# Values cut in two and set among the turns, keys before queries, the low-rank product before the last values

## Chip, cores and metric

One core of a Trainium2 chip runs the whole program. The metric is device time in microseconds (us) of that core, the median of several runs. Engines: TensorE (PE; its weight loads are listed as PEld), VectorE (DVE), ScalarE (ACT), GpSimd (POOL), and SyncE (SP), which issues the DMA transfers here.

## The reference

The input x is (2, 1024, 512), float32: 2048 tokens. What is computed:

```
xn = layernorm(x)
q  = xn @ Wq                      # 32 heads of 16
k,v = xn @ Wkv                    # 8 groups of 16 each, k and v interleaved
s  = softmax(causal(q k^T) / 4) v, @ Wo + bo
gate, up = xn @ gate_w + low rank (16), xn @ up_w + low rank (16)
g  = silu((silu(gate) * up) @ down_w + low rank (16))
out = x + s * g
```

## The kernel before

**Chunks.** The 2048 tokens are four chunks of 512 (c = 0 to 3); chunks 0 and 1 are batch 0, chunks 2 and 3 batch 1. For each chunk TensorE turns the normalised x (`turn_x`, four "turns" of four transposes each, line 1026). ScalarE rounds each turned block out of PSUM (`round_x`, line 1311) and copies it whole (`copy_x`, line 1318); for chunks 2 and 3 GpSimd forms the rest, x minus its rounding (`low_x`, line 631). Projections (`project`, lines 306 to 308) multiply in three products, high by high, high by low, low by high, and so need that rest of all four blocks of the chunk. Values (`value`, line 1062) and the product of x with the low-rank factors (`low`, line 1077) are plain float32 products of the whole copy. A key projection is block KEYS_BLOCK (4) of a chunk, a query projection one of blocks 0 to 3.

**Steps and slots.** Two streams are woven on every engine by `interleave`: attention, in slots, and background, in steps. A turn is one step, a projection, a low-rank product and the values of a chunk are four each. The 24 steps up to `("proj", 1, 0)` come ahead; the next 46 are spread over the 40 slots before the first attention round; then it is one step a slot. In this text steps are counted behind those 24: low(0) is steps 1 to 4 in both kernels. From slot 10 on each second slot or so holds a pair of score products (`score_pair`, line 1241) of query and key tiles, whose row maxima VectorE takes (`maximum`, lines 1809 and 1812) out of three PSUM banks; TensorE waits there for a bank to be read. After the last pair of a half VectorE splits the maxima (`split_max`, lines 1819 to 1825), and they are turned by TensorE (line 1248), copied by ScalarE (line 1553) and put into q by DMA (line 968).

**Banks.** Background results go to two PSUM banks in turn. `take_bank` makes TensorE wait until the result that lay in the bank before has been read: a turn by ScalarE's two copies, a value by its one copy (line 1343), a projection or low-rank product by ScalarE's rounding (line 1335 or 1354) and then VectorE's subtraction (line 1631 or 1636).

**Round trip by DRAM.** Projections, values and the low-rank product are stored to DRAM (lines 749, 754, 760) and read back in another layout. All issues stand in one order on the SP queue, and an SP wait holds what is behind it. `load_x_a` (line 768) waits for both stored low-rank products and issues six reads; the FFN's hidden stage needs them. The reads of k and q for attention group 1 (lines 949 and 952) wait for every projection up to the newest that they need, among them the keys of chunk 3; TensorE's score pairs of group 1 wait for those reads. They stand at slot 41 of the SP stream.

**Order around the change,** from step 1 (before): low(0) 1-4; value(0) 5-8; value(1) 9-12; turns of chunk 2, 13-16; queries (0,1) 17-20; keys of chunk 2, 21-24; value(2) 25-28; turns of chunk 3, 29-32; low(1) 33-36; queries (1,1) 37-40; keys of chunk 3, 41-44; value(3) 45-48; queries (0,2) 49-52; then the hidden stage (line 1099). SP's `background` stores each result behind its steps; `load_x_a` comes ahead of the store of the keys of chunk 3. In the GpSimd stream `low_query_weights(2)` and `low_of_low` (line 640, two operations) follow the four `low_x` of chunk 2.

Of the kernel before, what the change touches and what calls it, by code (L numbers as in the profile page):

```python
# [19 lines left out]
H, G = 32, 8  # L20
# [83 lines left out]
LEADING = [(c, blk) for c in range(2) for blk in (KEYS_BLOCK, 0)]  # L104
BESIDE = {2: (0, 1), 3: (1, 1)}
AFTER = [(0, 2), (1, 2), (0, 3), (1, 3)] + [(c, blk) for blk in range(NBLK - 1) for c in (2, 3)]
PROJECTED = LEADING + [p for c in BESIDE for p in (BESIDE[c], (c, KEYS_BLOCK))] + AFTER
BESIDE_HIDDEN = AFTER[1:]
QUERY_TILES = [[[0], [1], [2], [3]]] * 2

# [8 lines left out]
REST = 2  # L119


STEPS = dict(turn=1, proj=KT, value=TT, low=KT, hidden=2 * KT, down_fold=2, rest=REST, down=NH + 1, out=KT)

# [39 lines left out]
    return out_behind(t)  # L163


def bank_order():

    for c in range(2):
        for k in range(KT):
            yield "turn", c, k  # L170
    for c, blk in LEADING:
        yield "proj", c, blk
    yield "low", 0, 0
    for c in range(2):
        yield "value", c, 0
    for c in BESIDE:
        for k in range(KT):
            yield "turn", c, k
        if c == 3:
            yield "low", 1, 0  # L180
        yield ("proj", *BESIDE[c])
        yield "proj", c, KEYS_BLOCK
        yield "value", c, 0
    for c, blk in AFTER[:SOON]:
        yield "proj", c, blk
    for h in range(NH):
        for c in range(NCH):
            yield "hidden", h, c
            if c == 1:
                yield "proj", *AFTER[SOON + h]  # L190
    for h in range(NH):
        yield "down_fold", h, 0
    yield "rest", 0, 0
    for t in range(NT):
        yield "down", t, 0
        if out_behind(t) is not None:
            yield "out", out_behind(t), 0
    for t in range(NT - TT, NT):
        yield "out", t, 0
# [111 lines left out]
def layer(nc, x, Wq, Wkv, Wo, bo, gate_w, up_w, down_w, low_a, low_b, low_a_down, low_b_down, out):  # L311
# [5 lines left out]
    with ExitStack() as ctx:  # L317
# [203 lines left out]
        def wait_filled(engine, key):  # L521
            engine.wait_ge(filled, NUMBER[key] + 1)

        def projection(c, blk):
            return PROJECTED.index((c, blk))

        def read_out(kind, a, b):


            if kind == "down" and a < SPLIT_DOWN:  # L530
                return (y_left, a + 1), (y_right, a + 1)
            if kind == "out" and a < SPLIT_OUT:
# [5 lines left out]
            return dict(turn=(xT_copied if a else xT_lo, KT * a + b + 1), proj=(p_lo, (kind == "proj" and projection(a, b)) + 1), value=(v_copied, a + 1),  # L538
                        low=(x_a_lo, a + 1), down_fold=(d_lo, a + 1), down=(y_done, a + 1),
                        out=(r1_done, a + 1))[kind],  # L540

# [37 lines left out]
        def _(pool):  # L579
# [74 lines left out]
            def background():  # L654
# [15 lines left out]
                yield NUMBER_STEPS["value", NCH - 1, 0] - done  # L670
                done = NUMBER_STEPS["value", NCH - 1, 0]
                for i in range(2):
                    low_weight(0, i)
                for h in range(NH):
# [43 lines left out]
        def _(sp):  # L718
# [31 lines left out]

            def store_value(c):
                b, t0 = divmod(c * C, T)
                sp.wait_ge(v_copied, c + 1)
# [87 lines left out]
            def background():  # L841
# [7 lines left out]
                        load_first()  # L849
                yield STEPS["low"]  # L850
                store_x_a(0)
                for c in range(2):
                    yield STEPS["value"]
                    store_value(c)
                for c in BESIDE:
                    yield KT * STEPS["turn"]
                    for n in range(4 * (c - 2), 4 * (c - 2) + 4):
                        load_raw(n)
                    if c == 3:
                        yield STEPS["low"]  # L860
                        store_x_a(1)
                    yield STEPS["proj"]
                    store_projection(*BESIDE[c])
                    if c == 3:
                        load_x_a()
                    yield STEPS["proj"]
                    store_projection(c, KEYS_BLOCK)
                    yield STEPS["value"]
                    store_value(c)
                for c, blk in AFTER[:SOON]:  # L870
                    yield STEPS["proj"]
                    store_projection(c, blk)
# [142 lines left out]
        def _(pe):  # L1015
# [38 lines left out]
                        mm.then_inc(filled, 1)  # L1054
                    yield 1

            def value(c):
                pe.wait_ge(xT_copied, KT * (c + 1))
                out_ = take_bank(("value", c, 0))
                for t in range(TT):  # L1060
# [3 lines left out]
                    if t == TT - 1:  # L1064
                        mm.then_inc(filled, 1)
                    yield 1

# [117 lines left out]
            def background():  # L1185
# [4 lines left out]
                for c, blk in LEADING:  # L1190
                    yield from project(c, blk)
                yield from low(0)
                for c in range(2):
                    yield from value(c)
                for c in BESIDE:
                    for kt in range(KT):
                        yield from turn_x(c, kt)
                    if c == 3:
                        yield from low(1)
                    yield from project(*BESIDE[c])  # L1200
                    yield from project(c, KEYS_BLOCK)
                    yield from value(c)
                for c, blk in AFTER[:SOON]:
                    yield from project(c, blk)
                for h in range(NH):
# [97 lines left out]
        def _(act):  # L1303
# [8 lines left out]

            def copy_x(c, kt):
                if c >= 2:
                    wait_filled(act, ("value", c - 2, 0))
                elif c:
                    act.wait_ge(xT_lo, KT * c + kt + 1)
                nc.scalar.activation(xT[:, c % 2, kt], bank_of(("turn", c, kt))[:, :], ACT.Copy).then_inc(xT_copied, 1)
# [19 lines left out]
            def copy_value(c):  # L1338
                key = ("value", c, 0)
# [22 lines left out]
            def round_weight(h, i):  # L1362
                n, hp = 2 * h + i, rows[h]
                if n == 0:
                    wait_filled(act, ("value", NCH - 1, 0))
# [55 lines left out]
            def background():  # L1421
# [24 lines left out]
                    round_query_weights(blk)  # L1446
                yield STEPS["low"]
                round_x_a(0)
                for c in range(2):
                    yield STEPS["value"]  # L1450
                    if c:
                        root(3)
                    copy_value(c)
                for c in BESIDE:
                    for kt in range(KT):
                        yield STEPS["turn"]
                        round_x(c, kt)
                        copy_x(c, kt)
                    if c == 3:
                        yield STEPS["low"]  # L1460
                        round_x_a(1)
                    yield STEPS["proj"]
                    split_projection(*BESIDE[c])
                    yield STEPS["proj"]
                    split_projection(c, KEYS_BLOCK)
                    yield STEPS["value"]
                    copy_value(c)
# [112 lines left out]
        def _(dve):  # L1580
# [130 lines left out]
            def background():  # L1711
# [16 lines left out]
                normalise_x(3)  # L1728
                yield 2 * STEPS["value"]
                for c in BESIDE:  # L1730
                    for kt in range(KT):
                        yield STEPS["turn"]
                    if c == 3:
                        yield STEPS["low"]
                        low_of_x_a(1)
                    yield STEPS["proj"]
                    low_projection(*BESIDE[c])
                    yield STEPS["proj"]
                    low_projection(c, KEYS_BLOCK)
                    yield STEPS["value"]  # L1740
# [149 lines left out]
```

## Time and profile before

| | us |
|---|---|
| median of 3 runs | 932.41 (930.68 to 933.27) |
| the profiled execution, its own time | 935.35 |
| its span, first to last instruction | 933.6 |
| PE busy | 885.7 (95%) |
| DVE busy | 576.6 (62%) |
| ACT busy | 488.9 (52%) |
| POOL busy | 345.4 (37%) |

"Busy" is time in which an engine ran an instruction; waits are listed with what ended them. The granted clock of TensorE is 1.00 at full speed (2.4 GHz) and 0.50 at the lower level (1.2 GHz); its mean over the span is 0.984. Over the span the 16 DMA engines moved 137 GB/s.

### The profile page before, as it was taken

The page shows a single profiled execution, that of the slowest core. Times are in us where ns is not written, and L with a number is a line of the kernel's source. Part 1 is how long each engine was busy: PE and PEld are TensorE (multiplying, and loading weights), DVE is VectorE, ACT ScalarE, POOL GpSimd, SP SyncE. Part 2 cuts the span into 40 slices and gives each one's busy share as a digit, 9 for nine tenths or more (in the row PEclk, how much of TensorE's full clock was granted, in tenths as well). Part 3 has the DMA queues.
Part 4 walks back from the last instruction along what each step waited for, and adds up shares of the span by engine and source line. Part 5 has one row for each costly group of instructions (what it writes and reads, how often), then busy time and mean ns, then how long its engine had stood idle before and what let it go on. Part 6 is the DMA issues. An engine that isn't in the chain of part 4 may idle for free.

```text
span 933.6 us, 21793 instructions
## 1 busy us (share of the span) xinstructions
PE 885.7 (95%) x8415; PEld 641.2 (69%) x8415; DVE 576.6 (62%) x1674; ACT 488.9 (52%) x1002; POOL 345.4 (37%) x340
## 2 busy tenths in 40 slices
PE   3989799999999999999999999999999999999997
PEld 3754467676767676767677776665677777777885
DVE  7666466657566666666757566677766666661136
ACT  3441365656565656565656565656555454545211
POOL 4170236363636363635353545432021313130133
PEclk9998899999999999999999999997999999999999
DMA  8466525253525343434343434347465546434663
GB/s 278 158 190 170 150 71 154 61 148 84 144 72 149 81 143 85 135 87 130 94 130 91 132 97 133 97 136 222 128 224 158 160 138 186 160 98 136 211 207 134
DMA packets 143094, 129.80 MB, mean 139 GB/s; under 512 B 37360, under 2 KB 115920, under 8 KB 140816
## 3 DMA queue, kind: packets, MB, share of 16 engines
q1 hardware_dynamic: 142992, 128.41, 47.4%
q8 instruction: 68, 1.11, 0.5%
q14 instruction: 34, 0.28, 0.1%
HBM read 74.09 MB, written 53.74 MB: 137 GB/s over the span
## 4 chain that ended last, share of the span: by engine, by line
PE 86%; DVE 4%; DMA 3%; SPq 2%; ACT 2%; issue 2%; DVEq 0%; ACTq 0%
PE bank L1099 28%; PE bank L1142 15%; PE o L1277 14%; PE s L1241 9%; PE st L1260 8%; PE bank L306 3%; PE bank L307 2%; PE bank L308 2%; DMA sums<-scratch_o 1%; PE bank L1108 1%; PE bank L1077 1%; PE bank L1062 1%; SPq L968 1%; DMA scratch_k<-proj_hi 1%; PE bank L1122 1%
## 5 line engine op out<-in xcount | busy, mean ns | idle before, releaser
L1543 ACT ACTIVATE prob<-st 128x512 f32<-128x512 f32 (+1 forms) x640 | 323.3, 554 | 265.3 <-PE st L1260 263.7
L1809 DVE CUSTOM_DVE_ANT_0 junk<-s,mask 128x128 bf16<-128x128 f32 (+3 forms) x512 | 229.2, 487 | 81.4 <-PE s L1241 81.0
L1812 DVE TENSOR_REDUCE part_max<-s 128x1 f32<-128x512 f32 x256 | 164.1, 682 | 127.7 <-PE s L1241 127.2
L1241 PE MATMUL s<-k,q 64*128 64x512 f32 (+3 forms) x768 | 157.6, 376 | 15.4 <-DMA q<-scratch_q 6.6
L1099 PE MATMUL bank<-x_hi,w_hi 64*128 64x512 f32 (+1 forms) x704 | 151.0, 414 | 3.9 <-DVE proj_lo L1629 2.3
L604 POOL TENSOR_SCALAR_AFFINE_SELECT prob<-prob 128x512 f32<-128x512 f32 x128 | 81.1, 646 | 182.6 <-ACT prob L1543 182.5
L1277 PE MATMUL o<-prob,v 128*32 128x512 f32 (+3 forms) x1536 | 145.9, 498 | 0.0
L1099 PE MATMUL bank<-x_lo,w_hi 64*128 64x512 f32 (+1 forms) x704 | 143.6, 392 | 0.0
L1099 PE MATMUL bank<-x_hi,w_lo 64*128 64x512 f32 (+1 forms) x704 | 142.8, 390 | 0.0
L1260 PE MATMUL st<-q,k 64*128 64x512 f32 (+3 forms) x768 | 141.7, 347 | 1.0 <-ACT prob L1543 0.5
L1241 PEld LDWEIGHTS s<-k,q 64*128 64x128 f32 x768 | 80.9, 187 | 54.0 <-DVE part_max L1809 22.7
L1142 PE MATMUL bank<-down_hi,late_context_hid_in 64*128 64x256 f32 x1056 | 114.2, 287 | 0.3 <-DVE y L1669 0.3
L613 POOL TENSOR_TENSOR tanh<-tanh,hid 128x512 f32<-128x512 f32 (+1 forms) x44 | 56.6, 1287 | 149.1 <-DVE hid L1653 149.1
L1142 PEld LDWEIGHTS bank<-down_hi,late_context_hid_in 64*128 64x128 f32 x1056 | 93.3, 188 | 15.8 <-issue 15.0
L1099 PEld LDWEIGHTS bank<-x_hi,w_hi 64*128 64x128 f32 (+1 forms) x704 | 69.6, 182 | 42.8 <-issue 27.7
L1260 PEld LDWEIGHTS st<-q,k 64*128 64x128 f32 x768 | 85.1, 187 | 19.6 <-ACT prob L1543 8.3
L1277 PEld LDWEIGHTS o<-prob,v 128*32 128x32 f32 x1536 | 39.8, 110 | 64.2 <-issue 57.9
L621 POOL TENSOR_TENSOR hid_lo<-hid,tanh_hid_hi 128x512 fp32r<-128x512 f32 (+1 forms) x44 | 56.8, 1291 | 73.1 <-ACT tanh_hid_hi L1394 73.1
L1142 PE MATMUL bank<-down_lo,late_context_hid_in 64*128 64x256 f32 x528 | 79.1, 281 | 0.0
L1099 PEld LDWEIGHTS bank<-x_lo,w_hi 64*128 64x128 f32 (+1 forms) x704 | 69.5, 182 | 12.1
L1099 PEld LDWEIGHTS bank<-x_hi,w_lo 64*128 64x128 f32 (+1 forms) x704 | 69.8, 183 | 7.1
L615 POOL TENSOR_TENSOR hid<-tanh,hid 128x512 f32<-128x512 f32 (+1 forms) x44 | 56.9, 1293 | 3.5
(156 smaller groups left out, 1176.4 us busy)
## 6 DMA issues: line engine op xcount, KB each, us to landing
late_context_hid_in<-scratch_hid SPq DMA_DIRECT2D x16, 1408.0 KB, 6.4
q<-scratch_q SPq DMA_DIRECT2D x60, 200.0 KB
scratch_hid<-tanh_hid_hi SPq DMA_DIRECT2D x40, 256.0 KB, 2.4
scratch_hid<-hid_lo SPq DMA_DIRECT2D x40, 256.0 KB, 3.1
scratch_o<-o_sb SPq DMA_DIRECT2D x32, 256.0 KB
scratch_q<-proj_hi SPq DMA_DIRECT2D x30, 256.0 KB
k<-scratch_k SPq DMA_DIRECT2D x30, 192.0 KB
x_again<-in_L_attn_x SPq DMA_DIRECT2D x16, 256.0 KB, 4.9
```

What stands on the lines that cost most here:

```text
L604: ins = pool.affine_select(out=blk, in_=blk, compare_op=ALU.is_ge, fill=0.0, base=0, pattern=[[0, REP], [1, P]], channel_multiplier=-1)
L613: pool.tensor_tensor(th[0:hp, n % 2], th[0:hp, n % 2], hid[0:hp, n % 2], ALU.mult).then_inc(tanh_used, 1)
L615: pool.tensor_tensor(hid[0:hp, n % 2], th[0:hp, n % 2], hid[0:hp, n % 2], ALU.add).then_inc(hid_done, 1)
L621: pool.tensor_tensor(hid_l[0:hp, n % 2], hid[0:hp, n % 2], hid_h[0:hp, n % 2], ALU.subtract)\
L1099: mm = pe.matmul(bank[i][0:hp, :], w_[half, h % 2, i, kt, 0:hp], x_[half, c, kt], start=not cross and kt == 0 and w_ is wh and x_ is xh, s ...
L1142: mm = pe.matmul(bank[i][:, COLUMNS[i]], lhs[half], rhs[half, COLUMNS[i]], start=not cross and n == 0 and m == 0, stop=cross == 1 and n == ...
L1241: pe.matmul(sb_[(p + odd) % S_BANKS][:, 0:wd], q[half, g % 2, h // 2, qt * P:(qt + 1) * P], k[half, g % 2, k0:k0 + wd], start=True, stop=T ...
L1260: mm = pe.matmul(st[odd][:, col:col + q1 - q0], k[half, i % 2, kt * P:(kt + 1) * P], q[half, i % 2, h // 2, q0:q1], start=True, stop=True)
L1277: mm = pe.matmul(ob[32 * h:32 * h + 2 * HD, q0 % C:q0 % C + q1 - q0], v[:, i % 3, kt].rearrange("p a e -> p (a e)"), prob[:, job % 3, h, c ...
L1543: nc.scalar.activation(prob[:, job % 3, h, 0:JOB_COLS[j]], st[at % ST_BANKS][:, 0:JOB_COLS[j]], ACT.Exp, scale=float(HD) ** -0.5).then_inc ...
L1809: ins = dve.tensor_tensor_reduce(junk[:, n % S_BANKS, 0:wd], bank_[:, 0:wd], mask[:, C - wd:C], 1.0, LOWEST, ALU.add, ALU.max, part[:, h, ...
L1812: ins = dve.tensor_reduce(part[:, h, qt, dst:dst + 1], bank_[:, 0:wd], AX.X, ALU.max)
```

## The change

1. The values of a chunk are two parts of two steps, each with a bank, a copy and a count of its own. The values of chunk c - 1 stand among the turns of chunk c: one part behind each of the first two turns. Only value(0) stays ahead of the turns of chunk 2, and value(3) stays last.
2. In chunks 2 and 3 the key projection comes before the query projection, directly behind the last turn.
3. low(1) moves from behind the turns of chunk 3 to behind both its projections, ahead of value(3).
4. SP, ScalarE, VectorE and GpSimd follow the same order. `load_x_a` comes in SP's queue between the two parts of value(3), the store of a chunk's values behind its second part.

The order after: low(0) 1-4; value(0) 5-8; turn, value(1) part 0, turn, value(1) part 1, turn, turn, 9-16; keys of chunk 2, 17-20; queries (0,1) 21-24; the same with chunk 3 and value(2), 25-32; keys of chunk 3, 33-36; queries (1,1) 37-40; low(1) 41-44; value(3) 45-48; queries (0,2) 49-52.

```diff
-PROJECTED = LEADING + [p for c in BESIDE for p in (BESIDE[c], (c, KEYS_BLOCK))] + AFTER
+PROJECTED = LEADING + [p for c in BESIDE for p in ((c, KEYS_BLOCK), BESIDE[c])] + AFTER
...
+def turns_and_values(c):
+
+
+    for k in range(KT):
+        yield "turn", c, k
+        if k < 2:
+            yield "value", c - 1, k
+
...
     yield "low", 0, 0
-    for c in range(2):
-        yield "value", c, 0
+    for n in range(2):
+        yield "value", 0, n
     for c in BESIDE:
-        for k in range(KT):
-            yield "turn", c, k
-        if c == 3:
-            yield "low", 1, 0
+        yield from turns_and_values(c)
+        yield "proj", c, KEYS_BLOCK
         yield ("proj", *BESIDE[c])
-        yield "proj", c, KEYS_BLOCK
-        yield "value", c, 0
+    yield "low", 1, 0
+    for n in range(2):
+        yield "value", NCH - 1, n
...
# SP, background
-                for c in range(2):
-                    yield STEPS["value"]
-                    store_value(c)
+                yield 2 * STEPS["value"]
+                store_value(0)
                 for c in BESIDE:
-                    yield KT * STEPS["turn"]
+                    yield KT * STEPS["turn"] + 2 * STEPS["value"]
+                    store_value(c - 1)
                     for n in range(4 * (c - 2), 4 * (c - 2) + 4):
                         load_raw(n)
-                    if c == 3:
-                        yield STEPS["low"]
-                        store_x_a(1)
+                    yield STEPS["proj"]
+                    store_projection(c, KEYS_BLOCK)
                     yield STEPS["proj"]
                     store_projection(*BESIDE[c])
-                    if c == 3:
-                        load_x_a()
-                    yield STEPS["proj"]
-                    store_projection(c, KEYS_BLOCK)
-                    yield STEPS["value"]
-                    store_value(c)
+                yield STEPS["low"]
+                store_x_a(1)
+                yield STEPS["value"]
+                load_x_a()
+                yield STEPS["value"]
+                store_value(NCH - 1)
...
# TensorE, background
-                for c in range(2):
-                    yield from value(c)
+                for n in range(2):
+                    yield from value(0, n)
                 for c in BESIDE:
-                    for kt in range(KT):
-                        yield from turn_x(c, kt)
-                    if c == 3:
-                        yield from low(1)
+                    for kind, chunk, n in turns_and_values(c):
+                        yield from (turn_x if kind == "turn" else value)(chunk, n)
+                    yield from project(c, KEYS_BLOCK)
                     yield from project(*BESIDE[c])
-                    yield from project(c, KEYS_BLOCK)
-                    yield from value(c)
+                yield from low(1)
+                for n in range(2):
+                    yield from value(NCH - 1, n)
...
             def copy_x(c, kt):
                 if c >= 2:
-                    wait_filled(act, ("value", c - 2, 0))
+                    wait_filled(act, ("value", c - 2, 1))
...
-                nc.scalar.activation(vs[:, c % 2].rearrange("p g t e -> p t g e"),
-                                     bank_of(key)[:, :].rearrange("p (t g e) -> p t g e", t=TT, g=G),
+                nc.scalar.activation(vs[:, c % 2].rearrange("p g t e -> p t g e")[:, tiles],
+                                     bank_of(key)[:, :].rearrange("p (t g e) -> p t g e", t=TT, g=G)[:, tiles],
                                      ACT.Copy).then_inc(v_copied, 1)
```

## Rows read from the trace of the kernel before

**Rows 1.** Busy time in stretches of 20 us: engines, granted clock, DMA share, GB/s.
```profile
60.00:80.00 20.00, 15.97 (x71) 7.13 (x71) 9.42 (x25) 5.30 (x11) 6.17 (x5) 0.83 0.76 217
...
100.00:120.00 20.00, 14.91 (x121) 9.68 (x123) 8.54 (x36) 5.74 (x13) 3.71 (x5) 0.83 0.52 141
```

**Rows 2.** Waits of TensorE from 58 to 105.2 us: total, times, longest.
```profile
PE s L1241 <- DMA q<-scratch_q: 6.6, 1, 6.6
PE s L1241 <- DVE part_max L1812: 2.9, 3, 1.5
PE bank L1077 <- ACT xT L1318: 1.3, 1, 1.3
...
PE bank L1026 <- ACT xT L1318: 0.4, 1, 0.4
```

**Rows 3.** Stretches before and during low clock: columns PE, PEld, DVE, ACT, POOL, clock.
```profile
64.90:68.30 3.40, 2.03 (x13) 1.12 (x11) 1.27 (x5) 3.40 (x9) 2.38 (x2) 1.00 0.65 191
68.30:75.10 6.80, 6.25 (x16) 1.15 (x16) 1.29 (x2) 0.50 (x2) 3.79 (x4) 0.50 0.65 196
102.40:109.20 6.80, 4.13 (x19) 1.84 (x21) 0.51 (x4) 0.74 (x2) 1.23 (x2) 0.50 0.54 145
662.20:665.60 3.40, 3.40 (x33) 3.35 (x32) 1.90 (x6) 0.96 (x2) 0.00 (x0) 0.50 0.32 105
```

**Rows 4.** Timeline of TensorE: start, length, line, operands, count, idle before.
```profile
48.58 0.66 PE L1026 MATMUL bank<-ident,ring 128*128 128x128 f32 x4
...
61.33 0.33 PE L1241 MATMUL s<-k,q 64*128 64x128 f32 x2 [1.53 <-DVE part_max L1812]
...
66.90 0.63 PE L1026 MATMUL bank<-ident,ring 128*128 128x128 f32 x4 [0.35 <-ACT xT L1318]
68.85 1.92 PE L1077 MATMUL bank<-xT,prob 128*32 128x512 f32 x4 [1.32 <-ACT xT L1318]
...
75.40 1.05 PE L1077 MATMUL bank<-xT,prob 128*32 128x512 f32 x4
...
86.63 0.40 PE L308 MATMUL bank<-x_hi,wk_lo 128*128 128x512 f32 x1
...
105.07 0.47 PE L1241 MATMUL s<-k,q 64*128 64x128 f32 x2 [6.55 <-DMA q<-scratch_q]
```

**Rows 5.** Timeline of ScalarE.
```profile
49.77 0.59 ACT L1318 ACTIVATE xT<-bank 128x512 f32<-128x512 f32 x1
...
67.58 0.26 ACT L1553 ACTIVATE neg_rows<-s 32x128 f32<-32x128 f32 x1
```

**Rows 6.** Timeline of GpSimd.
```profile
47.25 4.99 POOL L631 TENSOR_TENSOR x_lo<-xT,x_hi 128x512 fp32r<-128x512 f32 x4 [10.44 <-ACT xT L1318]
...
53.63 6.32 POOL L640 TENSOR_TENSOR low_b<-prob,low_b 16x1376 fp32r<-16x1376 f32 x2
```

**Rows 7.** Timeline of VectorE.
```profile
43.57 1.92 DVE L1610 TENSOR_SCALAR ring<-ring,mean_var,small 128x512 f32<-128x512 f32 x4
...
56.87 3.12 DVE L1825 TENSOR_TENSOR neg_pad<-neg_max,neg_pad 128x16 fp32r<-128x16 f32 x1
59.91 0.68 DVE L1631 TENSOR_TENSOR proj_lo<-bank,proj_hi 128x512 fp32r<-128x512 f32 x1
...
77.12 0.68 DVE L1636 TENSOR_TENSOR prob<-bank,prob 64x512 fp32r<-64x512 f32 x1 [0.57 <-ACT prob L1354]
```

**Rows 8.** Timeline of the SP queue: when issues start, and how long they take.
```profile
77.83 1.15 SPq L760 DMA_DIRECT2D scratch_low<-prob  x2
...
85.33 4.46 SPq L768 DMA_DIRECT2D low_x<-scratch_low  x6
...
99.07 0.79 SPq L949 DMA_DIRECT2D k<-scratch_k  x2
```

**Rows 9.** Line 760: landing times. Line 768: issues, min/median/max ns.
```profile
DMA to landing us min/median/max: 2.3/2.6/3.4
...
L768 SPq DMA_DIRECT2D low_x<-scratch_low x6: 412/437/1200, 85.3 to 89.4; - x6
```

More of the change, by code:

```diff
@@ L119 @@
 REST = 2
-STEPS = dict(turn=1, proj=KT, value=TT, low=KT, hidden=2 * KT, down_fold=2, rest=REST, down=NH + 1, out=KT)
+STEPS = dict(turn=1, proj=KT, value=TT // 2, low=KT, hidden=2 * KT, down_fold=2, rest=REST, down=NH + 1, out=KT)
 SPLIT_DOWN, SPLIT_OUT = 12, NT // 2
@@ L537, in read_out @@
                 return (gate_read, NCH * a + b + 1), (up_read, NCH * a + b + 1)
-            return dict(turn=(xT_copied if a else xT_lo, KT * a + b + 1), proj=(p_lo, (kind == "proj" and projection(a, b)) + 1), value=(v_copied, a + 1),
+            return dict(turn=(xT_copied if a else xT_lo, KT * a + b + 1), proj=(p_lo, (kind == "proj" and projection(a, b)) + 1), value=(v_copied, 2 * a + b + 1),
                         low=(x_a_lo, a + 1), down_fold=(d_lo, a + 1), down=(y_done, a + 1),
@@ L669, in background @@
                 low_query_weights(3)
-                yield NUMBER_STEPS["value", NCH - 1, 0] - done
-                done = NUMBER_STEPS["value", NCH - 1, 0]
+                yield NUMBER_STEPS["value", NCH - 1, 1] - done
+                done = NUMBER_STEPS["value", NCH - 1, 1]
                 for i in range(2):
@@ L752, in store_value @@
                 b, t0 = divmod(c * C, T)
-                sp.wait_ge(v_copied, c + 1)
+                sp.wait_ge(v_copied, 2 * c + 2)
                 sp.dma_start(s["v"][:, b].rearrange("g p t e -> p g t e")[:, :, t0 // P:t0 // P + TT],
@@ L1055, in project, with value @@
                     yield 1
-            def value(c):
+            def value(c, n):
                 pe.wait_ge(xT_copied, KT * (c + 1))
-                out_ = take_bank(("value", c, 0))
-                for t in range(TT):
+                out_ = take_bank(("value", c, n))
+                for t in range(n * TT // 2, (n + 1) * TT // 2):
                     for kt in range(KT):
@@ L1063, in value @@
                                        wkv[:, kt, :, 1], start=kt == 0, stop=kt == KT - 1)
-                    if t == TT - 1:
+                    if t % 2:
                         mm.then_inc(filled, 1)
@@ L1336, in split_projection, with copy_value @@
                 ins.then_inc(p_hi, 1)
-            def copy_value(c):
-                key = ("value", c, 0)
+            def copy_value(c, n):
+                key = ("value", c, n)
+                tiles = slice(n * TT // 2, (n + 1) * TT // 2)
                 wait_filled(act, key)
@@ L1364, in round_weight @@
                 if n == 0:
-                    wait_filled(act, ("value", NCH - 1, 0))
+                    wait_filled(act, ("value", NCH - 1, 1))
                     act.wait_ge(xT_lo_late, 2 * KT)
@@ L1448, in background @@
                 round_x_a(0)
-                for c in range(2):
+                for n in range(2):
                     yield STEPS["value"]
-                    if c:
-                        root(3)
-                    copy_value(c)
+                    copy_value(0, n)
+                root(3)
                 for c in BESIDE:
[L1455 to L1461, printed above, removed]
+                    for kind, chunk, n in turns_and_values(c):
+                        yield STEPS[kind]
+                        if kind == "turn":
+                            round_x(chunk, n)
+                            copy_x(chunk, n)
+                        else:
+                            copy_value(chunk, n)
+                    yield STEPS["proj"]
+                    split_projection(c, KEYS_BLOCK)
                     yield STEPS["proj"]
                     split_projection(*BESIDE[c])
-                    yield STEPS["proj"]
-                    split_projection(c, KEYS_BLOCK)
+                yield STEPS["low"]
+                round_x_a(1)
+                for n in range(2):
                     yield STEPS["value"]
-                    copy_value(c)
+                    copy_value(NCH - 1, n)
                 for i in range(2):
@@ L1730, in background @@
                 for c in BESIDE:
[L1731 to L1735, printed above, removed]
+                    yield KT * STEPS["turn"] + 2 * STEPS["value"]
+                    yield STEPS["proj"]
+                    low_projection(c, KEYS_BLOCK)
                     yield STEPS["proj"]
                     low_projection(*BESIDE[c])
-                    yield STEPS["proj"]
-                    low_projection(c, KEYS_BLOCK)
-                    yield STEPS["value"]
+                yield STEPS["low"]
+                low_of_x_a(1)
+                yield 2 * STEPS["value"]
                 for c, blk in AFTER[:SOON]:
```

## The prediction

> **What bounds the kernel now.** The page comes first: TensorE is busy 95% of the span, so a change pays only if it takes idle time or half-speed time from TensorE. The view by stretches says where there is any near the change: from 60 to 80 and from 100 to 120 us TensorE works 16.0 and 14.9 of 20 us, and the clock averages 0.83 in both [rows 1]. The view of waits names the idle time [rows 2]: 6.6 us for the q reads of group 1, 2.9 us in three waits for a score bank (the longest, 1.53, ends at 61.33 [rows 4]), and 1.3 + 0.35 us for ScalarE's copies around the turns of chunk 3. The clock rows give the rest [rows 3]: a low clock from 68.3 to 75.1, behind a stretch in which TensorE was busy 2.03 of 3.4 us with turns and small pairs, and another from 102.4 to 109.2, behind the wait for q. In the first TensorE was busy 6.25 us at half speed, which cost 6.25 / 2 = 3.1 us; in the second 4.13, which cost 2.1.
>
> What sets the end of this stage is the wait for q, which ends at 105.07 [rows 4]. Everything behind it is dense TensorE work, so I take the shift of that moment as the shift of the end. Before, it is the end of a chain: the keys of chunk 3 end on TensorE at 86.63 + 0.40 = 87.03 (step 44) [rows 4], SP is busy with the six low-rank reads from 85.33 on [rows 8], stores the keys, waits for them to land, and issues the reads at 99.07 [rows 8]; the first pair starts 6.0 us later. From step 44 to that pair: 18.0 us, of which TensorE works from 87.03 to 105.07 - 6.55 = 98.5 at steps 45 to 52, 11.5 us.
>
> **The sum to step 44.** Steps 1 to 44 hold the same TensorE instructions in both kernels (low(1) takes the place of the keys of chunk 3 at its end), so only waits and clock differ.
>
> Taken away. The wait of 1.32 ahead of low(1) and the 0.35 between turns: 1.7. The wait of 1.53 for a score bank: VectorE stood in a 16-column subtraction (line 1825) for 3.12 us, until GpSimd's two operations of line 640 ended at 53.63 + 6.32 = 59.95 [rows 6, 7]. In the new order the eighth pair is some 2.5 us later by the wait below, the subtraction then meets only the end of them, and the wait goes: 1.5. The half clock of 68.3 to 75.1: 3.1. Together 6.3 us.
>
> Added, first: the key projection stands directly behind the fourth turn and needs GpSimd's rest of it. Before, the queries (0,1) or low(1) covered that work. The last turn of chunk 2 ended at 48.58 + 0.66 = 49.24, its copy at 49.77 + 0.59 = 50.36, 1.1 us later [rows 4, 5]; GpSimd takes 4.99 / 4 = 1.25 a block [rows 6], and one block may still be in work: 1.1 + 1.25 + some 0.2 = 2.6 us. In chunk 3 ScalarE also copies the turned maxima in between (0.26 [rows 5]): 2.8. These are waits with nothing beside them, as score pairs stand behind the projection in TensorE's own order: 5.4.
>
> Second: value(2) part 0 takes the bank of the queries (0,1), with one turn between. ScalarE needs 0.6 and VectorE 0.68 [rows 7] behind the projection, VectorE perhaps after a pair of maxima; less the turn of 0.6, that is 0.8 to 1.4, I take 1.1. The second part of values waits for ScalarE's copy of the first behind one turn: 0.15 each, 0.3. The four added copies are ScalarE work of under 0.6 each at 52% busy, beside TensorE's values: nothing else.
>
> Third, the clock. It fell at 68.3 behind turns with short waits between them, 3.4 - 2.03 = 1.4 us of idle time in all [rows 3]; the new waits are 2.6 and 2.8 us, each behind two turns. So I expect a fall at each. What one costs: nothing, if the clock stays; half of 3.4 = 1.7, as at 662.2 to 665.6, where it came back after that time; 3.1, as at 68.3. Dense projections follow here, as dense work does at 662, and a part of the wait lies in the low time, so I take 1.6 each, 3.2.
>
> Step 44 then ends at 87.03 - 6.3 + 5.4 + 1.4 + 3.2 = 90.7. Without falls it is 87.5; with falls of 3.1 each, 93.7.
>
> The Trainium skill (TensorE: Matmul & The Clock Gate, the table of terms ahead of Part 1) prices low clock as its whole time by the share of pulses left out. By that the removed fall is 6.8 / 2 = 3.4 in place of 3.1, since it counts idle time too, and the sum would be 0.3 less.
>
> **From step 44 to the reads of group 1.** The keys of chunk 3 now end at step 36, some 10 us earlier, so their store has landed when the reads want it. But `load_x_a` stands directly ahead of those reads in SP's queue: it is due at step 47, the reads one slot on, and it waits for the store of low(1), which is now step 44. What is queued behind its wait are the reads of k and q, and TensorE waits for them. The chain, from the rows of low(1) before: TensorE ended at 75.40 + 1.05 = 76.45 and SP issued the store at 77.83, 1.4 later [rows 4, 7, 8]. The second store of the two starts 0.6 on and lands in 2.3 to 3.4, median 2.6 [rows 9]. Six reads took 4.46 us to issue with stores queued [rows 8]; at their median of 0.44 they would take 2.7 [rows 9]. The queue is emptier now: 3.3. Then the reads, 6.0 to the first pair, plus what the six transfers ahead of them take: 0 to 1.5, I take 0.8. Sum 1.4 + 0.6 + 2.6 + 3.3 + 6.0 + 0.8 = 14.7; bounds 13.0 and 17.2.
>
> So the wait ends at 90.7 + 14.7 = 105.4 against 105.07: 0.3 us later. TensorE reaches it at 90.7 + 11.5 = 102.2 instead of 98.5, so it idles 3.2 us, not 6.6: part of that wait is moved forward into the two waits for GpSimd. The fall of the clock behind it I leave as it is, 2.1. The profiled execution would take 935.35 + 0.3; it stands 2.9 above the median, and the same shift on the median, 932.41, gives **932.7 us**. Other moves (stores of values, v reads, raw weights) keep their place within a few steps and end well before their users: nothing, while SP is not full.
>
> **The rivals.** A measurement of this kernel tells about 0.3%, 2.8 us, from no change.
>
> Faster, the clock holds. If it stays at full speed through both new waits, step 44 ends at 87.5, the wait for q at 102.2, 2.9 earlier: 929.5 us. For it: the idle 1.53 before 61.33 lay between dense values and brought no fall. Against: the new waits are nearly twice as long and behind turns. Also a chain of 13.0 alone would give 1.4 less. Chance 0.22.
>
> Slower, the clock stays low. Each fall lasts as from 68.3 to 75.1 and takes 3.1: step 44 at 93.7, the pair at 108.4, 3.3 later: 935.7 us; with the longer chain, 938. It decides as soon as both falls together cost more than 5.7. For it: the fall at 68.3 met four busy-looking steps and did not end. Against: those were low(1), with 32 columns of weights, and here it is the three-product projections. Chance 0.25.
>
> VectorE against GpSimd. GpSimd's first rest of chunk 2 moves to about 43.3, where VectorE normalises chunk 3 (43.57 to 45.49) [rows 7]; before, GpSimd stood still there until 47.25 [rows 6]. If one holds the other as line 640 held line 1825, the first maxima start up to 1.25 later, and TensorE with them: 934.0 us. Chance 0.10, inside no change. The Trainium skill (GPSIMD Engine Reference, Specifications) names such contention for VectorE operations in a two-port mode or with two SBUF inputs; by that rule the normalisation could be one of them. The trace agrees for the second kind: the 3.12 us of line 1825.
>
> That the keys' earlier store does free the reads is excluded by the order of SP's queue, unless the low-rank store lands at once.
>
> **How the numbers follow.** The forecast has 0.43. Together with the third rival, no change has 0.53, faster 0.22, slower 0.25. The range takes both clock cases and most of the chain's bounds: from 928.8 (no fall and a chain 0.7 us short) to 936.8 (two long falls and a chain a microsecond long).
>
> **What would show it.** On TensorE, ahead of the first product of each key projection, a wait of 2.6 to 2.8 us put down to GpSimd's x_lo. Low clock behind each of them, shorter than 6.8 us. On VectorE, line 1825 near 59 under 1.5 us. On SP, the six low-rank reads directly ahead of k and q of group 1, starting about 95 us. TensorE's wait for q, 3 to 4 us, ending near 105. I am wrong if the key projections start without a wait, if the reads of k go out before 95, or if the time behind 110 us is not shifted as the wait is.

## The result and the profile after

The changed kernel takes 940.87 us (937.62 to 941.64, 4 runs), the kernel before 931.54 (928.51 to 933.27, 4 runs): ratio 1.0079, 95% interval 1.0053 to 1.0105. The change costs 0.8% by that ratio, 7.4 us (4.9 to 9.8 by its interval); the two medians alone lie 9.3 us apart. The forecast was 932.7 and the range ended at 936.8. The profiled executions: 940.55 (span 938.6) against 935.35 (span 933.6).

Timeline of TensorE in the kernel before, then in the changed one. The first row of each is the start of low(0), the same instruction; it is 1.06 us earlier in the second trace, so positions are best taken from there. Line numbers in views of the changed kernel are its own: 314 to 316 are the projections, 639 and 648 GpSimd's rests and its two long operations, 1069 the values, 1084 low, 1248 the score pairs, 1620 the normalisation of x, 1833 the long subtraction. In the kernels of the experiments they shift by a line or two.

```profile
34.24 3.63 PE L1077 MATMUL bank<-xT,prob 128*32 128x512 f32 x16
```

```profile
33.18 3.63 PE L1084 MATMUL bank<-xT,prob 128*32 128x512 f32 x16
...
46.60 0.38 PE L1248 MATMUL s<-k,q 64*128 64x256 f32 x2 [1.66 <-DVE part_max L1817]
...
52.80 0.80 PE L314 MATMUL bank<-x_hi,wk_hi 128*128 128x512 f32 x1 [2.52 <-POOL x_lo L639]
...
67.09 1.13 PE L1069 MATMUL bank<-wkv,xT 128*128 128x128 f32 x8 [1.07 <-DVE proj_lo L1641]
...
77.11 0.79 PE L314 MATMUL bank<-x_hi,wk_hi 128*128 128x512 f32 x1 [3.30 <-POOL x_lo L639]
...
92.87 1.91 PE L1084 MATMUL bank<-xT,prob 128*32 128x512 f32 x8
...
111.04 0.47 PE L1248 MATMUL s<-k,q 64*128 64x128 f32 x2 [4.96 <-DMA q<-scratch_q]
```

Four new waits stand where [rows 4] had three others: for VectorE at the first maxima, for GpSimd ahead of both key projections, for a bank at value(2). The first pair of group 1 comes 111.04 - 33.18 = 77.9 us behind the start of low(0), before 105.07 - 34.24 = 70.8 [rows 4]: 7.0 us more, of the 7.4 us that the ratio gives. The two stretches of low clock on the way and the one behind the wait for q, in the changed kernel, and then one near 640 us in the kernel before and in the changed one (columns as in [rows 3]; the last two are the DMA share and GB/s):

```profile
51.99:62.23 10.24, 9.44 (x23) 5.45 (x23) 3.03 (x13) 0.60 (x1) 8.20 (x4) 0.51 0.66 173
75.87:82.70 6.83, 5.59 (x13) 3.22 (x13) 1.29 (x2) 0.00 (x0) 2.42 (x2) 0.52 0.68 183
110.10:116.80 6.70, 5.76 (x29) 3.19 (x31) 1.29 (x8) 0.74 (x2) 1.22 (x2) 0.52 0.37 89
```

```profile
638.30:648.50 10.20, 10.20 (x51) 5.32 (x51) 7.24 (x27) 4.80 (x10) 0.64 (x1) 0.50 0.80 230
```

```profile
646.00:652.80 6.80, 6.80 (x39) 3.36 (x40) 5.39 (x21) 3.44 (x7) 0.63 (x1) 0.51 0.90 277
```

At half speed TensorE was busy 9.44 and 5.59 us: half of that, 4.7 and 2.8 us, is lost, where the old order lost 3.1 [rows 3]. The fall behind the wait for q costs 5.76 / 2 = 2.9 here and cost 2.1 before. The stretch near 640 us, far from the change, differs the other way between these two executions, by 1.7 us. So the wait for q ends 6.0 us later by the clock of the traces, and the spans differ by 6.0 + 0.8 - 1.7 = 5.1, measured 5.0.

SP's queue in the changed kernel, around the reads of group 1:

```profile
96.17 1.41 SPq L768 DMA_DIRECT2D scratch_low<-prob  x2
...
99.68 2.69 SPq L776 DMA_DIRECT2D low_x<-scratch_low  x6
102.49 0.81 SPq L956 DMA_DIRECT2D k<-scratch_k  x2
103.34 1.48 SPq L959 DMA_DIRECT2D q<-scratch_q  x4
```

From step 44 (92.87 + 1.91 = 94.78): 1.4 to the store, 3.5 to the first low-rank read, 2.8 for the six, then 8.55 from the first read of k to the pair at 111.04. Before, that last piece was 6.0 [rows 8].

VectorE and then GpSimd in the changed kernel, at the normalisation of chunk 3, and VectorE at the subtraction of [rows 7]:

```profile
42.50 3.84 DVE L1620 TENSOR_SCALAR ring<-ring,mean_var,small 128x512 f32<-128x512 f32 x4
...
64.49 0.17 DVE L1833 TENSOR_TENSOR neg_pad<-neg_max,neg_pad 128x16 fp32r<-128x16 f32 x1
```

```profile
42.44 1.28 POOL L639 TENSOR_TENSOR x_lo<-xT,x_hi 128x512 fp32r<-128x512 f32 x1 [6.68 <-ACT xT L1325]
44.80 1.26 POOL L639 TENSOR_TENSOR x_lo<-xT,x_hi 128x512 fp32r<-128x512 f32 x1 [1.08 <-ACT xT L1325]
```

The normalisation took 3.84 us in place of 1.92, with two GpSimd rests beside it; the subtraction took 0.17 in place of 3.12, clear of GpSimd.

### The profile page after: what moved, and what is told of

Its sections match the earlier page's. It is cut to its first block, busy times and chain, and to the rows that moved or that the text cites. A ratio compares the mean times of both kernels' runs of the same rounds, so it can differ in the third digit from the quotient of the medians.

```text
span 938.6 us, 21803 instructions
## 1 busy us (share of the span) xinstructions
PE 887.9 (95%) x8415; PEld 646.3 (69%) x8415; DVE 575.8 (61%) x1674; ACT 489.2 (52%) x1006; POOL 345.2 (37%) x340
## 4 chain that ended last, share of the span: by engine, by line
PE 88%; DVE 4%; DMA 2%; issue 2%; ACT 2%; SPq 1%; POOL 1%; DVEq 0%; ACTq 0%
PE bank L1106 27%; PE bank L1149 15%; PE o L1284 14%; PE s L1248 10%; PE st L1267 8%; PE bank L314 3%; PE bank L316 3%; PE bank L315 3%; PE bank L1115 1%; DVE ring L1620 1%; DMA q<-scratch_q 1%; PE s L1255 1%; PE bank L1084 1%; PE bank L1129 1%; DVE junk L1817 1%
```

## The experiments

Ratios are to the kernel before on the same chip, with 95% intervals. The difference of two such ratios is uncertain by about 0.3%. The first four separate what is new in the changed kernel.

**queries_first.** In `bank_order`, and the same on each engine:

```diff
+        yield ("proj", *BESIDE[c])
         yield "proj", c, KEYS_BLOCK
-        yield ("proj", *BESIDE[c])
```

> The changed kernel with the query projection of chunks 2 and 3 ahead of the key projection again; values among the turns and low(1) behind stay. Theory (the loss is the two waits for GpSimd's rests and the low clock behind each): both waits (2.5 and 3.3 us) and both low-clock stretches (about 7 us lost) go, the wait for q ends 11 to 13 us earlier than in the changed kernel, near 99; time 925 to 930 us, faster than before. Rival 1 (the loss is the low-rank reads ahead of the reads of k and q): at most 2 us less than the changed kernel, 938 or more. Rival 2 (the clock falls behind turns with values between them whatever follows): waits go, one low stretch stays, 931 to 934.

931.78 us, ratio 0.9980 (0.9959 to 1.0000). Its TensorE timeline:

```profile
61.73 1.13 PE L1069 MATMUL bank<-wkv,xT 128*128 128x128 f32 x8 [2.19 <-DVE proj_lo L1641]
...
70.84 0.47 PE L314 MATMUL bank<-x_hi,wq_hi 128*128 128x512 f32 x1 [0.83 <-ACT xT L1325]
...
102.34 0.47 PE L1248 MATMUL s<-k,q 64*128 64x128 f32 x2 [5.09 <-DMA q<-scratch_q]
```

Both waits for GpSimd are gone, and with them the loss: the wait for q ends 8.7 us earlier (111.04 to 102.34), 1% less time. Ahead of the wait for q one low stretch of 3.4 us is left, at 63.3, behind a wait of 2.19 for a bank. The theory is right that these waits and falls are the loss, but its 925 to 930 us and its wait ending near 99 did not come; the time and the one stretch left are those of the second rival (931 to 934). Whether that stretch comes of the values between turns, as the rival says, or of the wait for the bank, this run does not tell. A gain over the kernel before is not shown: the interval ends at 1.0000.

**filler.** Useless products in the two waits:

```diff
+                    for _ in range({2: 11, 3: 14}[c]):
+                        pe.matmul(ob[:, :], xh[:, 0, 0, 0:P], xh[:, 0, 0], start=True, stop=True)
                     yield from project(c, KEYS_BLOCK)
```

> The changed kernel with 11 and 14 products of 512 columns (0.23 us each) of no use, written to the unused bank o, put on TensorE ahead of the key projections of chunks 2 and 3, where it waits for GpSimd; the output is not touched. Theory (more than half of the loss is the low clock, brought on by the idle waits): the key projections start when they did, the clock stays at 1.00 through 50 to 83 us, the wait for q ends some 7 us earlier, near 104; time 932 to 935 us. Rival 1 (the waits themselves are the loss, the clock follows from something else): low stretches stay and the time stays at 938 to 941.

935.78 us, ratio 1.0026 (1.0007 to 1.0046). TensorE's timeline, and its row by stretches:

```profile
50.29 2.79 PE L1206 MATMUL o<-x_hi 128*128 128x512 f32 x11
53.08 0.50 PE L314 MATMUL bank<-x_hi,wk_hi 128*128 128x512 f32 x1
...
104.35 0.47 PE L1250 MATMUL s<-k,q 64*128 64x128 f32 x2 [4.67 <-DMA q<-scratch_q]
```

```profile
40.00:103.90 63.90, 54.67 (x298) 36.43 (x296) 37.11 (x108) 20.80 (x41) 22.06 (x15) 1.00 0.65 176
```

The first key product starts at 53.08, no earlier than at 52.80, yet the clock is 1.00 up to the wait for q, which ends 6.7 us earlier. From the start of low(0) to the end of step 44, in the kernel before, the changed kernel and filler:

```profile
34.24:87.03 52.79, 47.70 (x252) 28.42 (x251) 32.64 (x95) 15.36 (x30) 19.93 (x13) 0.94 0.57 170
```

```profile
33.18:94.78 61.60, 51.52 (x252) 31.71 (x251) 31.85 (x95) 16.11 (x33) 20.02 (x13) 0.86 0.52 157
```

```profile
33.42:88.38 54.96, 50.54 (x277) 32.64 (x276) 31.93 (x95) 16.12 (x33) 20.22 (x13) 1.00 0.58 176
```

The same 252 matrix instructions take 61.60 us in the changed kernel; with 25 more that fill the waits, and no low clock, they take 54.96. The two falls cost 6.6 us of this stretch. In time, filling the waits without shortening them takes back 1.0079 - 1.0026 = 0.53%, about 5 us, with 2 to 8 allowed by the intervals; the time is 0.8 above the theory's range. It is not one trace alone: the mean granted clock of the ten runs of filler was 0.983 to 0.990, of the four of the changed kernel 0.977 to 0.983. So idle time in these two waits brings the falls on, and in the traces they cost 6.6 us where the pair came 7.0 later than before.

**reads_first.**

```diff
                 yield STEPS["low"]
                 store_x_a(1)
-                yield STEPS["value"]
-                load_x_a()
-                yield STEPS["value"]
+                yield 2 * STEPS["value"]
+                load_x_a()
                 store_value(NCH - 1)
```

> The changed kernel with the six low-rank reads moved behind the reads of k and q of group 1 in SP's queue. Theory (those reads stand behind them for 2.7 us and share the DMA engines with them): TensorE's wait for q of 5.0 us shrinks to under 1, as the reads go out near 98; 935 to 937 us. Rival (the reads wait for stores, not for the queue): the wait stays above 3 us, 939 or more. Third way: the hidden stage then waits for the low-rank reads, a new wait near 112 that takes up to 4 us back.

935.30 us, ratio 1.0028 (1.0005 to 1.0050). SP's queue and the waits of TensorE from 34 to 125 us:

```profile
98.55 1.40 SPq L768 DMA_DIRECT2D scratch_low<-prob  x2
100.08 1.01 SPq L955 DMA_DIRECT2D k<-scratch_k  x2
101.13 1.48 SPq L958 DMA_DIRECT2D q<-scratch_q  x4
102.66 2.86 SPq L776 DMA_DIRECT2D low_x<-scratch_low  x6
```

```profile
PE bank L314 <- POOL x_lo L639: 6.0, 2, 3.3
...
PE bank L1114 <- DMA low_x<-scratch_low: 1.1, 1, 1.1
```

The wait for q has gone from the list, and 1.1 us for the low-rank reads is new (the third way, in part). The time is inside the theory's range. The reads of k go 0.1 us behind the end of the store's issue, not 4.9: it was the queue. The clock has a part in this too:

```profile
47.60:51.00 3.40, 3.36 (x14) 2.58 (x15) 1.20 (x7) 0.38 (x1) 0.00 (x0) 0.53 0.52 186
...
100.00:114.00 14.00, 13.74 (x95) 9.24 (x93) 9.15 (x29) 8.49 (x17) 4.35 (x5) 1.00 0.87 173
```

The fall behind the wait for q (2.9 us) is gone with the wait, and a new one (1.7 us) stands behind the 1.66 us wait for the first maxima, a wait that brought no fall in the changed kernel, in queries_first or in filler. 5.0 - 1.1 + 2.9 - 1.7 = 5.1 us, against 1.0079 - 1.0028 = 0.51%, 4.8 us.

**norm_alone.**

```diff
                 pool.wait_ge(xT_copied, KT * c + kt + 1)
+                if c == 2 and kt == 0:
+                    pool.wait_ge(xn_ready, NCH)
```

> The changed kernel, but GpSimd's first rest of chunk 2 waits until VectorE has normalised chunk 3. Theory (the two hold each other where they overlap: 3.84 us of normalisation in place of 1.92, and a wait of 1.66 us of TensorE for the first maxima): normalisation about 1.9 us, that wait under 0.3, everything behind it 1 to 1.7 us earlier; 938.5 to 940 us. Rival (the normalisation is longer for another reason): no shift, 3.8 us stay.

940.33 us, ratio 1.0070 (1.0044 to 1.0097): in time not told apart from the change. In the trace, VectorE, then TensorE:

```profile
44.40 1.91 DVE L1622 TENSOR_SCALAR ring<-ring,mean_var,small 128x512 f32<-128x512 f32 x4
```

```profile
35.08 3.63 PE L1086 MATMUL bank<-xT,prob 128*32 128x512 f32 x16
...
111.51 0.47 PE L1250 MATMUL s<-k,q 64*128 64x128 f32 x2 [5.37 <-DMA q<-scratch_q]
```

1.91 us again, the wait of 1.66 is gone, and from low(0) to the pair it is 76.4 us, not 77.9: 1.4 less, as expected; the time is 0.3 above the theory's range. The collision is shown; what it is worth, only the trace says.

**rest_on_dve.** The rests of chunks 2 and 3 on VectorE:

```diff
-                        low_x(c, kt)
...
+            def late_x(c, kt):
+                dve.wait_ge(xT_hi, KT * c + kt + 1)
+                dve.wait_ge(xT_copied, KT * c + kt + 1)
+                dve.tensor_tensor(xl[:, c, kt], bank_of(("turn", c, kt))[:, :], xh[:, c, kt], ALU.subtract).then_inc(xT_lo_late, 1)
...
+                        if kind == "turn":
+                            late_x(chunk, n)
```

A turn's bank now comes free only behind this subtraction.

> The changed kernel with the rests of chunks 2 and 3 taken on VectorE straight from the bank (0.69 us each) and not on GpSimd (1.25). Theory (the wait is the last copy, 1.1 us, plus the last rest): the waits ahead of the key projections fall from 2.5 and 3.3 to 1.8 and 2.2 us, and the normalisation is 1.9 us; the clock may still fall; 936 to 940 us. Rival (VectorE, which also takes the maxima, becomes the bound): waits for maxima and banks grow by more than the waits shrink, 941 or more.

944.24 us, ratio 1.0133 (1.0082 to 1.0183): the rival. TensorE's waits, 34 to 125 us:

```profile
PE bank L1032 <- DVE x_lo L1632: 4.9, 1, 4.9
PE bank L314 <- DVE x_lo L1632: 4.8, 2, 2.8
```

The waits ahead of the keys shrink from 5.8 to 4.8 us together, where the theory had 4.0, but the first rest stands behind the normalisation in VectorE's order, and the second turn waits 4.9 us for the bank that it holds; low clock stands beside it from 46.0 on.

**keys_only** and **low_only** put one part of the change into the kernel before:

```diff
# keys_only
+        yield "proj", c, KEYS_BLOCK
         yield ("proj", *BESIDE[c])
-        yield "proj", c, KEYS_BLOCK
         yield "value", c, 0
...
# low_only
+        yield ("proj", *BESIDE[c])
+        yield "proj", c, KEYS_BLOCK
         if c == 3:
             yield "low", 1, 0
-        yield ("proj", *BESIDE[c])
-        yield "proj", c, KEYS_BLOCK
...
+                        yield STEPS["value"] // 2
                         load_x_a()
+                        yield STEPS["value"] // 2
```

The last lines are SP's: low_only also moves the six low-rank reads, into the middle of value(3), as in the changed kernel.

> The kernel before with only the key projections of chunks 2 and 3 put ahead of the query projections. Theory: in chunk 2 a wait for GpSimd of 2.5 us and a low-clock stretch behind it, in chunk 3 none, as low(1) covers the rests; the keys are stored earlier and the wait for q shrinks from 6.6 to under 2; both about cancel, 930 to 935 us. Rival (the keys ahead are the whole loss of the change): 938 or more.

932.33 us, ratio 1.0001 (0.9981 to 1.0021). Timeline, clock and waits of TensorE:

```profile
52.19 0.79 PE L306 MATMUL bank<-x_hi,wk_hi 128*128 128x512 f32 x1 [3.02 <-POOL x_lo L631]
```

```profile
51.20:61.40 10.20, 9.21 (x23) 5.26 (x23) 2.97 (x13) 0.60 (x1) 8.41 (x4) 0.50 0.55 154
```

```profile
PE s L1241 <- DMA q<-scratch_q: 3.8, 1, 3.8
```

The clock from the end of that stretch to the wait for q:

```profile
61.60:105.60 44.00, 36.02 (x195) 22.27 (x197) 24.40 (x66) 14.38 (x27) 9.30 (x8) 1.00 0.64 185
```

One wait of 3.0 and one long fall of 9.21 / 2 = 4.6 come in chunk 2 and none in chunk 3. Against them the old fall at 68.3 (3.1) is gone, the wait for maxima at the eighth pair is down from 1.5 to 0.3, and the wait for q is 2.8 us shorter: they cancel, as expected, though 3.8 is left of that wait and not 2. The waits of 0.4 and 1.3 us that stood ahead of the old fall are still there, without a fall.

> The kernel before with only low(1) moved behind both projections of chunk 3, and the low-rank reads between the halves of value(3). Theory: the wait of 1.3 us ahead of low(1) goes, the bank of the second last turn costs under 1, the low clock of 68 to 75 us goes or costs 1.7 instead of 3.1; the low-rank reads now stand ahead of the reads of k and q, wait for q ends some 15 to 16 us behind low(1), near 99 to 101; 927 to 931 us. Rival (the moved low-rank reads are what made the changed kernel slow): 935 or more.

930.97 us, ratio 0.9978 (0.9963 to 0.9994). TensorE at turns and queries of chunk 3, and its waits:

```profile
66.00:73.00 7.00, 6.14 (x25) 3.43 (x25) 3.49 (x8) 2.48 (x6) 5.24 (x5) 1.00 0.69 201
```

```profile
PE s L1243 <- DMA q<-scratch_q: 8.2, 2, 7.3
```

No low clock between the turns and the queries, and a wait for q of 7.3 in place of 6.6. Alone, moving low(1) with the reads gains 0.2% and the key order nothing. In the changed kernel both stand together and take the cover from chunk 3's rests; the two without the cut values were not tried. **before_reads_first** moves the six reads in the kernel before:

```diff
                     store_projection(*BESIDE[c])
-                    if c == 3:
-                        load_x_a()
                     yield STEPS["proj"]
                     store_projection(c, KEYS_BLOCK)
                     yield STEPS["value"]
+                    if c == 3:
+                        load_x_a()
                     store_value(c)
```

> The kernel before with only the six low-rank reads moved in SP's queue from ahead of the store of the keys of chunk 3 to behind the reads of k and q of group 1. Theory (they hold the key store by 1.4 us and its landing by their traffic): the reads go out 4 to 5 us earlier, the wait for q shrinks from 6.6 to 1.5 to 2.5 us; 927 to 930 us. Rival (the 7 us to landing are the store's own): wait above 5 us, 931 or more.

931.51 us, ratio 0.9986 (0.9966 to 1.0006): the rival's time, with a wait between the two. Waits of TensorE:

```profile
PE s L1241 <- DMA q<-scratch_q: 4.5, 2, 4.0
...
PE bank L1108 <- DMA low_x<-scratch_low: 1.7, 1, 1.7
```

The long wait falls from 6.6 to 4.0 and 1.7 comes back at the hidden stage; what holds the reads now is the store of the keys: SP waits 5.1 us for it to land.

**Combinations.** `qf_reads_first` is queries_first with the edit of reads_first; `before_two` is before_reads_first with GpSimd's two long operations moved; `best` is qf_reads_first with norm_alone and that move; `all_three` is the changed order with filler, reads_first and norm_alone.

```diff
-                pool.wait_ge(wq_lo, 3)
+                pool.wait_ge(wq_lo, 4)
...
                         low_query_weights(2)
-                        low_of_low()
                 low_query_weights(3)
+                low_of_low()
```

> The changed kernel with the queries ahead of the keys again and the six low-rank reads behind the reads of k and q of group 1. Theory (waits for GpSimd and the order of SP's queue are two separate losses): TensorE's wait for q (5.1 us with queries first alone) goes, and the low clock behind it; a wait of about 1 us for the low-rank reads takes its place; 924 to 928 us. Rival (the reads of k and q are held by the stores of the late keys of chunk 3, steps 37 to 44, not by the queue): the wait stays above 3 us, 930 or more.

930.17 us, ratio 0.9981 (0.9962 to 1.0001): the wait for q is down to 0.2, but the low-rank reads now cost 2.9, and the clock fell twice:

```profile
46.40:53.20 6.80, 6.34 (x24) 4.70 (x25) 3.75 (x17) 1.75 (x4) 0.88 (x1) 0.53 0.40 151
63.50:70.30 6.80, 6.18 (x25) 5.10 (x26) 2.29 (x8) 1.22 (x3) 1.14 (x1) 0.53 0.61 194
```

Theory and rival both fail: the queue was the holder, but the time is the rival's and the 5 us did not arrive. The two falls stand at the waits of 1.7 (maxima, from the collision at the normalisation) and 2.1 us (bank, from the split values). queries_first has the same waits and fell only once ahead of its wait for q, for 3.4 us; what decided that in either execution was not tried.

> The kernel before with the six low-rank reads behind the reads of k and q and GpSimd's two operations on the low-rank weights behind the rests of chunk 3. Theory: the wait of 1.5 us at 61 and the 3.1 us of line 1825 go, the rest as with the reads alone: 928 to 931 us. Rival (nothing but the clock's phase decides): same as the reads alone, 931 to 933.

930.54 us, ratio 0.9968 (0.9951 to 0.9984), inside the theory's range. The wait at 61 is 0.3 and no low clock is left ahead of 98 us.

> The changed kernel, order as changed, with the fill of TensorE in both waits for GpSimd, the low-rank reads behind the reads of k and q, and GpSimd's first rest behind the normalisation. Theory (the losses add: 5 for the clock, 5 for the reads, 1.5 for the normalisation, some of it taken back by the wait for the low-rank reads): 928 to 932 us. Rival (they overlap, so one of them brings nothing once the others are gone): 934 or more.

928.84 us, ratio 0.9951 (0.9931 to 0.9970), inside the theory's range. The single edits were worth 0.53, 0.51 and 0.09%, together 1.13, so their sum gives 0.9966. Within the noise the losses add.

> The changed kernel with queries first, the six low-rank reads behind the reads of k and q, GpSimd's first rest of chunk 2 behind the normalisation of chunk 3, and GpSimd's two operations on the low-rank weights behind the rests of chunk 3. Theory (each named wait is a loss of its own): no wait of TensorE over 1 us from 40 to 98 us, so at most one low-clock stretch there, a wait of 3 us for the low-rank reads stays; 922 to 926 us. Rival (low clock comes whenever turns are spread, waits or not): clock low at two places before 98, 929 or more.

926.04 us, ratio 0.9922 (0.9898 to 0.9947), the lowest median of all, though its interval overlaps that of all_three. Waits of up to 1.3 us are left ahead of 95 us (the theory had none over 1), and no fall. Its clock from 40 to 95 us, and its waits:

```profile
40.00:95.00 55.00, 48.85 (x273) 31.90 (x271) 34.97 (x108) 20.80 (x41) 21.95 (x15) 1.00 0.66 195
```

```profile
PE s L1249 <- DMA q<-scratch_q: 3.1, 2, 1.8
PE bank L1116 <- DMA low_x<-scratch_low: 1.8, 1, 1.8
```

## Why the prediction was wrong, step by step

**Right.** The waits for GpSimd: 2.52 and 3.30 us for 2.6 and 2.8. The bank at value(2): 1.07 for 1.1; the 0.3 for the second parts of the values did not show. The wait at 61 and the long subtraction went. The six reads stood ahead of those of group 1, and the wait for q shrank (4.96, forecast 3.2) without its end coming earlier. The spans moved by 5.0 us and that moment by 6.0, so taking the one for the other was sound to a microsecond, with luck: elsewhere 0.8 us of low clock came on top and 1.7 fell away. Filler, the changed order without falls, took 54.96 us from low(0) to the end of step 44; the prediction without falls has 87.5 - 34.24 = 53.3, and with the 1.7 us of the collision below 55.0. So the rest of the sum to step 44 was right.

**Wrong, and the step that failed: what one fall of the clock costs, 1.6 us each, 3.2.** They cost 4.7 and 2.8 by TensorE's busy time at half speed, together 7.5, and 6.6 by the comparison with filler. The prediction took the short fall at 662 us as its pattern because dense products follow there as here. They did follow, and the clock stayed low for 10.2 us behind the first wait and 6.8 behind the second, where it expected less than 6.8 each time. The longest stretch in the trace of before, 10.2 us near 638, was not among the rows that the prediction rests on, so the upper bound of 3.1 was no bound. From low(0) on, step 44 ended after 61.6 us and not after 90.7 - 34.24 = 56.5, 5.1 late: 3.4 is the clock (6.6 in place of 3.2), 1.7 the collision below. The filler run shows that this term is real and what brings it on. The rival "the clock stays low" had the mechanism, and with 3.1 a fall it was still too low for the first.

**Missing in the sum: the collision of VectorE and GpSimd.** It was a rival with a chance of 0.10 and 1.25 us; it took 1.92 us of VectorE and 1.66 of TensorE, and the 3.84 us came again in queries_first, filler and reads_first. It depends on the order, not on luck, and belonged in the sum. The Trainium skill (GPSIMD Engine Reference, Specifications) names contention of GpSimd with VectorE instructions in a two-port mode or with two SBUF inputs. The trace agrees that there is contention: norm_alone brought the normalisation back to 1.91. It has one tensor input, so it would be of the first kind; in which mode it ran, no run shows.

**Too small: the traffic of the six reads,** 0.8 us. From the first read of k to the pair it was 8.55 us in place of 6.0: 2.5. The chain from step 44 was 16.3 and not 14.7, within its bounds of 17.2 (its terms at their upper ends add up to 17.4). That the six transfers cause it is likely, not shown: with them directly ahead this piece was 8.4 to 9.1 us in five more runs, with them directly behind 6.7 and 7.1 in before_reads_first and before_two, but 8.6 in best.

**Offset by an early start.** The changed kernel's stage began 1.06 us earlier in its trace, so absolute positions understate the shift: 6.0 by the clock of the trace, 7.0 from low(0) on. From low(0) the forecast was 0.3, and the miss of 6.7 is 3.4 (clock), 1.7 (collision) and 1.6 (chain).

The pricing of TensorE: Matmul & The Clock Gate (Terms) in the Trainium skill, low time by the share of pulses left out, gives an estimate of (10.24 + 6.83) / 2 = 8.5 us. The traces do not bear it out here: the busy time at half speed gives 7.5, and the filler run gave back 6.6 in the trace and about 5 in the time of all runs.

## What to carry to other kernels

When a reorder puts a consumer right behind its producer, price the wait twice: its own length, and a clock fall behind it. As its bound take half of the longest stretch at low clock that the trace shows anywhere, 5.1 us here; the falls measured in the changed stage cost 1.7 to 4.7 us. What hid the producer's helper engine before (here a query projection in one chunk, low(1) in the other) may be removed by two moves that were harmless one by one (1.0001 and 0.9978). In a queue with one order, read what stands directly ahead of the transfer that is waited for; here taking six reads out of the way was worth 0.51%, the fall behind the wait included, against 0.53% for the two falls ahead of it.

## What was not expected of the hardware

- Once fallen, TensorE's clock stayed low for 10.2 us although TensorE was busy for 9.4 of them with dense products; the same stretch of 10.2 is in keys_only and norm_alone, while falls of 3.4 us are in queries_first and others.
- Behind each of the nine waits of 2.0 to 3.3 us for a rest ahead of a key projection that stayed unfilled, in five kernels, the clock was low. Shorter waits did not decide it: 1.66 us for the first maxima was followed by a fall in reads_first and qf_reads_first and by none in the changed kernel, queries_first and filler.
- Eleven and fourteen useless products in waits of 2.5 and 3.3 us kept the clock at 1.00 and took back about 5 us in time (6.6 in the trace), about what the waits themselves last (5.8).
- Two GpSimd subtractions of 1.28 and 1.26 us beside four normalisations on VectorE doubled the time of these, 1.92 to 3.84 us, while their own stayed at the usual 1.25.
